# A graph layer on one core: six instead of four relations as seven half-size products, edge work re-placed

## What is computed

```python
xn = layernorm(x)
# graph part: relational mean of neighbours, R = 8
u = xn @ root + bias
for r in range(8):
    mask = (edge_type == r)
    sums = segment_sum(xn[src] * mask, dst); cnt = segment_sum(mask, dst)
    u = u + (sums / max(cnt, 1)) @ weight[r]
z = concat([u, xn], 1) @ w_gate + b_gate
h = tanh(u) * z + xn * (1 - z)
# linear attention of 16 heads: q, k, v, g, o products of 1024 x 1024
x = x + h + attention(xn)
# one LSTM cell per row: three of four gates, their x half
x = x + lstm(layernorm(x))
```

## Time and profile before

| | us |
|---|---|
| median of three runs | 2176.46 |
| fastest run | 2169.57 |
| the profiled execution | 2178.85 |
| its span, first to last instruction | 2177.1 |
| busy: TensorE | 2123.1 |
| busy: VectorE | 1307.1 |
| busy: GpSimd | 715.4 |
| busy: ScalarE | 538.5 |
| mean granted TensorE clock, of full | 0.989 |

### The profile page before, as it was taken

One profiled execution on the slowest core, in us unless ns is written; L12 is line 12 of the kernel. 1 busy time (PEld: TensorE's weight loads), 2 busy tenths in 40 slices (PEclk: granted clock), 3 DMA queues, 4 the chain that ended last, 5 costly groups with the idle time before them and its releaser, 6 DMA issues.

```text
span 2177.1 us, 25376 instructions
## 1 busy us (share of the span) xinstructions
PE 2123.1 (98%) x9562; PEld 1711.9 (79%) x9562; DVE 1307.1 (60%) x1737; ACT 538.5 (25%) x749; POOL 715.4 (33%) x631
## 2 busy tenths in 40 slices
PE   7789899989999999999999999999999999999999
PEld 6667677778888888888877778889988888788887
DVE  5565979756666666676666566773355658534233
ACT  4334354511111111100121211112232313321121
POOL 1404002026556556453635445541212353000000
PEclk9899999999999999999999999999999999999999
DMA  7887676769588988793978888964169988604102
GB/s 274 298 282 239 226 248 210 259 176 330 194 286 314 302 300 301 266 304 96 332 256 283 276 275 292 310 214 159 65 185 267 283 286 266 179 16 131 55 30 80
DMA packets 248145, 497.69 MB, mean 229 GB/s; under 512 B 39441, under 2 KB 71872, under 8 KB 248022
## 3 DMA queue, kind: packets, MB, share of 16 engines
q1 hardware_dynamic: 165782, 279.20, 39.0%
q0 software_dynamic: 65248, 191.13, 26.5%
q10 hardware_dynamic: 16992, 25.73, 3.7%
HBM read 403.60 MB, written 133.45 MB: 247 GB/s over the span
## 4 chain that ended last, share of the span: by engine, by line
PE 87%; DVE 5%; DMA 4%; issue 2%; ACT 1%; POOL 1%; SPq 0%; ACTq 0%; POOLq 0%; DVEq 0%
PE acc L1414 70%; PE acc L1385 10%; PE acc L1409 5%; DMA ax_d<-aTraw 1%; DMA y_d<-made 1%; POOL runs L2386 1%; PE acc L1322 1%; DMA xr<-in_x 1%; DVE Wlo L1710 1%; DMA made<-y_d 1%; PE misc L1307 1%; PE tp L1269 0%; DMA runs<-code_d,run_row 0%; DVE res L1781 0%; PE acc L1422 0%
## 5 line engine op out<-in xcount | busy, mean ns | idle before, releaser
L1414 PE MATMUL acc<-Whi,aThi 128*128 128x512 f32 (+1 forms) x2232 | 882.1, 395 | 0.7 <-DVE A L2139 0.6
L1414 PE MATMUL acc<-Whi,aTlo 128*128 128x512 f32 (+1 forms) x2232 | 879.1, 394 | 0.0
L1414 PE MATMUL acc<-Wlo,aThi 128*128 128x512 f32 (+1 forms) x2232 | 876.5, 393 | 0.0
L2406 POOL DMA_INDIRECT ring<-y_d,edge x390 | 477.8, 1225 | 429.2 <-DVE U L2009 138.8
L1414 PEld LDWEIGHTS acc<-Whi,aTlo 128*128 128x128 f32 (+1 forms) x2232 | 413.7, 185 | 103.5
L1414 PEld LDWEIGHTS acc<-Wlo,aThi 128*128 128x128 f32 (+1 forms) x2232 | 414.4, 186 | 102.4
L1414 PEld LDWEIGHTS acc<-Whi,aThi 128*128 128x128 f32 (+1 forms) x2232 | 413.6, 185 | 103.3 <-DVE A L2139 1.1
L1710 DVE TENSOR_TENSOR Wlo<-Wraw,Whi 128x1024 fp32r<-128x1024 f32 x176 | 218.9, 1249 | 156.4 <-ACT Whi L1440 152.8
L1385 PE MATMUL acc<-Whi,aThi 128*128 128x512 f32 (+2 forms) x560 | 230.5, 412 | 36.0 <-DVE Wlo L1710 12.1
L2009 DVE SCALAR_TENSOR_TENSOR U<-ring,edge,U 128x1024 f32<-128x1024 f32 x180 | 230.4, 1280 | 23.6 <-DMA ring<-y_d,edge 23.1
L2009 DVE SCALAR_TENSOR_TENSOR odd<-ring,edge,odd 128x1024 f32<-128x1024 f32 x170 | 217.6, 1280 | 36.7 <-DMA ring<-y_d,edge 36.2
(11 more groups left out here) (209 smaller groups left out, 1520.8 us busy)
## 6 DMA issues: line engine op xcount, KB each, us to landing
Wraw<-in_L_gnn_weight SPq DMA_DIRECT2D x80, 512.0 KB, 7.7
y_d<-res SPq DMA_DIRECT2D x80, 256.0 KB, 3.4
Whraw<-in_L_gnn_weight SPq DMA_DIRECT2D x24, 512.0 KB, 7.1
y_d<-made ACTq DMA_DIRECT2D x32, 256.0 KB
Wraw<-in_L_gnn_w_gate SPq DMA_DIRECT2D x16, 512.0 KB, 7.4
y_d<-made ACTq DMA_DIRECT2D x32, 252.0 KB
ring<-y_d,edge POOLq DMA_INDIRECT x390, 6.3
aTraw<-ax_d SPq DMA_DIRECT2D x4, 1250.0 KB, 9.7
```

The source lines that it names most:

```text
L1414: mm = nc.tensor.matmul(to, a[:, k, rows(i)], b[:, s % 2, k, :], start=start, stop=stop)
L2406: pool.indirect_dma_start(ring[:, j % RING, :], None, a, bass.IndirectOffsetOnAxis(ap=index, axis=0), bounds_check=top - 1, oob_is_err=Fal ...
```

## The change

`SEVEN` now holds six relations. There are 210 block units in place of 140, and four Y stages in place of eight; units in all are 474 in place of 444. All places that follow from it (junctions of AL, BE and DE, `SPREAD`, `SWAP`) keep their distance to their stages. `RIGHT_AT` moves from units 25 to 30 to units 44 to 50. The edges' preparation up to the reading of runs stays at its units; what follows is stretched from 61/32 to 183/64 of a unit, starts at unit 57 in place of 55, and the pieces of the tables stand 1.8 units apart in place of 0.5. GpSimd makes all its row sums before the edge codes. The sums' first half lies on units 214 to 277 (63 units, to unit 7 of the first `V_`) in place of 144 to 223 (79); the second half on 277 to 347 (70) in place of 223 to 317 (94). Both still end in the last `G_`. `y_d` keeps its two halves of four relations.

```diff
@@ -83,14 +83,14 @@
-SEVEN = list(range(HALF_R))
+SEVEN = list(range(6))
...
-STAGE += [(Y_, r, h) for r in range(HALF_R, R) for h in range(2)]
+STAGE += [(Y_, r, h) for r in range(len(SEVEN), R) for h in range(2)]
@@ -225,9 +225,10 @@
-AL_LAST, BE_FIRST, DE_FIRST = HALF_R - 1, HALF_R, STAGE.index((DE_, 0, 0))
+AL_LAST, BE_FIRST, DE_FIRST = len(SEVEN) - 1, len(SEVEN), STAGE.index((DE_, 0, 0))
-SPREAD = [(3, None, 31), (0, POS[AL_LAST, 4], 35), (1, LAST[AL_LAST], 41), (2, None, 43)]
+SPREAD = [(3, None, FIRST[AL_LAST] + 1), (0, POS[AL_LAST, 4], FIRST[AL_LAST] + 5), (1, LAST[AL_LAST], FIRST[BE_FIRST] + 1),
+          (2, None, FIRST[BE_FIRST] + 3)]
@@ -308,17 +309,17 @@
-RIGHT_AT = (25, 28, 29, 30)
+RIGHT_AT = (44, 46, 48, 50)
...
-SENDS_AT = (104, 131)
+SENDS_AT = (132, 193)
...
-    return divmod(440 + (8 * (q - 36) + k) * 61 // 32, 8)
+    return divmod(462 + (8 * (q - 36) + k) * 183 // 64, 8)
@@ -359,8 +360,8 @@
-SUMS_FROM = (place(Y_, 0, 4, HALF_R), place(R_, 0, 3))
-SUMS_TO = (place(R_, 0, 3), place(G_, 1, 7))
+SUMS_FROM = (place(Y_, 0, 4, len(SEVEN)), place(V_, 0, 7))
+SUMS_TO = (place(V_, 0, 7), place(G_, 1, 7))
@@ -1673,7 +1674,7 @@
-                            if (q, k) == edge_at(43 + 15 * h + t // 2 * 3 + t % 2, 5):
+                            if (q, k) == edge_at(44 + 20 * h + t // 2 * 3 + t % 2, 5):
                                 rank_signs(h, t)
@@ -2298,27 +2299,27 @@
-                        if (q, k) == edge_at(36 + h, 6):
+                        if (q, k) == edge_at(36 + 2 * h, 6 - 4 * h):
                             run_half(h)
-                    if (q, k) == edge_at(38, 2):
+                    if (q, k) == edge_at(39, 2):
                         run_keys()
...
-                            if (q, k) == edge_at(41 + 15 * h + t // 2 * 3 + t % 2, 1):
+                            if (q, k) == edge_at(42 + 20 * h + t // 2 * 3 + t % 2, 1):
                                 top_of(h, t)
-                        if (q, k) == edge_at(58 + 15 * h, 1):
+                        if (q, k) == edge_at(58 + 20 * h, 1):
                             ranks_whole(h)
...
-                            if (q, k) == edge_at(58 + 15 * h, 4 + 2 * piece):
+                            if (q, k) == edge_at(59 + 20 * h, 5 * piece):
                                 tables_weights(h, piece)
@@ -2470,15 +2471,13 @@
-            for t in (1, 2):
+            for t in range(1, T):
                 rows_sum(t)
             edge_codes()
...
-            for t in range(3, T):
-                rows_sum(t)
```

More of the change, by code:

```diff
@@ L1331, in beside @@
                     turn_x(TURN_AT[q])
-                if q == place(Y_, 0, 4, HALF_R) and k == 2:
+                if q == place(Y_, 0, 4, len(SEVEN)) and k == 2:
                     any_bad()
@@ L2300, in _ @@
                     for h in range(2):
-                        if (q, k) == edge_at(36 + h, 6):
+                        if (q, k) == edge_at(36 + 2 * h, 6 - 4 * h):
                             run_half(h)
-                    if (q, k) == edge_at(38, 2):
+                    if (q, k) == edge_at(39, 2):
                         run_keys()
                     for h in range(2):
-                        if (q, k) == edge_at(38 + h, 6):
+                        if (q, k) == edge_at(39 + h, 6):
                             hold_half(h)
@@ L2309, in _ @@
                         for t in range(T):
-                            if (q, k) == edge_at(41 + 15 * h + t // 2 * 3 + t % 2, 1):
+                            if (q, k) == edge_at(42 + 20 * h + t // 2 * 3 + t % 2, 1):
                                 top_of(h, t)
-                        if (q, k) == edge_at(58 + 15 * h, 1):
+                        if (q, k) == edge_at(58 + 20 * h, 1):
                             ranks_whole(h)
-                        if (q, k) == edge_at(58 + 15 * h, 2):
+                        if (q, k) == edge_at(58 + 20 * h, 2):
                             tables(h)
                         for piece in range(4):
-                            if (q, k) == edge_at(58 + 15 * h, 4 + 2 * piece):
+                            if (q, k) == edge_at(59 + 20 * h, 5 * piece):
                                 tables_weights(h, piece)
-                    if (q, k) == (place(Y_, 0, 2, HALF_R), 5):
+                    if (q, k) == (place(Y_, 0, 2, len(SEVEN)), 5):
                         columns_over()
-                    if (q, k) == (place(Y_, 0, 5, HALF_R), 2):
+                    if (q, k) == (place(Y_, 0, 5, len(SEVEN)), 2):
                         which_path()
```

## The result

| | before | after |
|---|---|---|
| median beside each other, us | 2177.85 | 2158.73 |
| ratio, with its 95% interval | | 0.9904 (0.9885 to 0.9923) |
| the profiled execution, us | 2178.85 | 2150.63 |
| its span, us | 2177.1 | 2148.8 |
| block stages, from the first to the first Y unit, us | 460.8 (140 units) | 611.0 (210 units) |

The change takes about 1% off; the prediction was 2119 with 2100 to 2155, and the median lies above that range.

A forecast was written before the change was run, and what follows sets the result against it. TensorE, busy 98% of the span, was taken as the bound. 2177.1 - 27 (products) - 33 (pauses) + 0 (edge sums) = 2117 us of span, so 2119 us, range 2100 to 2155.

The forecast's parts named there:

- Products: TensorE's matmuls: two relations change from Y stages to seven half-size products each, 27 us less, bounds 20 and 27.
- Pauses: TensorE's pauses in the block stages, before 471.2 us: four causes eased, 33 us less, bounds 5 and 50.
- GpSimd's order: First 23 block units: row sums ahead of the edge codes end SyncE's and VectorE's waits, 10 us back, bounds 0 and 17.
- The right-hand differences: Second and third block stretches: moving RIGHT_AT later avoids VectorE's wait for the store of x's sides, 10 us, bounds 3 and 14.
- The runs: VectorE's 6.9 us wait for the runs of codes shrinks with 15 units' lead instead of 13: 5 us, bounds 0 and 6.
- The tables: Block stages: table pieces spread to 1.8 units apart no longer hold up evictions, 8 of 7 + 9 us, bounds 2 and 13.
- The edge sums: Ordinary stages: gather-and-add steps squeezed to 1.80 and 1.88 us still stay hidden, 0 us, bounds 0 and 40.
- the ring's pace away from a stage's start: Ordinary stages after a stage's first four units: five gathers in flight allow a step every 1.56 us, so the plan is met.
- B: Rival, chance 0.25: the ring of gathers falls behind by a few per cent, 1.92 us a step, TensorE waits 22 us, 2141 us.
- C: Rival, chance 0.08: the ring runs throughout at 2.2 us a step as at a stage's start, TensorE waits 137 us, 2256 us.
- A: The forecast case, chance 0.55: products and pauses give 60 us and the edge sums stay hidden, 2119 us, range 2102 to 2135.
- D: Rival, chance 0.12: block-stage pauses stay because they are the DMA's; only products and 5 us count, 2147 us.

The follow-up runs named there:

- six places: Changed kernel with six places in the ring of gathers in place of five; median 2113.03 us, ratio to before 0.9703.
- four places: Changed kernel with four places in the ring of gathers in place of five; 2245.6 us in one run.
- seven places: Changed kernel with seven places in the ring of gathers in place of five; median 2108.09 us, ratio to before 0.9686.

## Why the prediction was wrong

**Products, 27 us: right.** Every BE, GA and DE stage from unit 70 on takes 27.9 us, with no excess. No run isolates this term; it closes the account.

**Pauses, 33 us: right in kind, too small; 44.8 in the trace of after, 40 to 48 by the traces with the same block stages.** By item:

1. GpSimd's order, 10 foreseen: 8 us between the traces (8.8 us at units 17 and 18 before, 0.9 after), 3 to 9 when undone or done alone. Row sum 3 starts at 34.32 us, before 45 as required.
2. The right-hand differences, 10 foreseen: 10.4 us went at the junction of AL and BE (14.6 at units 35 to 42 of before, 4.2 at 59 to 62 of after). The cause named holds in the trace of before, whose chain runs through the wait of the earlier trace rows and ScalarE behind it; of the 4.2 us that stayed, the chain of after is the storing and loading for seeds that was foreseen to stay. **The cure was not the one named**: with `RIGHT_AT` at its old units the wait returned and no time with it, and with everything else of the edges put back units 30 to 58 stayed free of pauses as well. What is left is that two more AL stages put the junction and its spreads 20 units later, away from the wait. That was not tried by itself, nor was `RIGHT_AT` moved alone in the kernel before.
3. The runs, 5 foreseen: 9.2 us were lost at units 59 to 61 of before, and in the trace of after the runs cost nothing. That was luck in part, since "no wait for runs" did not hold: six places waited 11.4 us for them, before itself 6.9. With the old places the loss there was 8 to 12 us more.
4. The tables, 8 foreseen: all 16.3 us went. The old pace brings 8.5 of them back, the first half's nearly whole; the other 8 most likely went with the place of the second half's tables. I had read their price, 7 + 9 us, and taken only half of it back. Items 3 and 4 together are what the spread is for: undoing it costs 16 to 20 us at the runs and the tables, less than the products give.

**The edge sums, 0 us (bounds 0 and 40): wrong, +43.7 us.** The failed step is the ring's pace away from a stage's start, (6.2 + 1.3 + 0.3) / 5 = 1.56 us. It was mis-sized in three terms. From an add's end to the next issue it is not 0.3 but 1.34 us: 1.49 us where GpSimd was still issuing another gather (121 of the steps 40 to 194, 1.29 us an issue), and 0.80 us even where it was free. A gather lands in 6.8, not 6.2 us, with five always in flight. And VectorE begins 0.4 us after the landing on average (at once in two steps of three, later where splits and evictions come between). (6.8 + 1.23 + 1.34 + 0.4) / 5 = 1.95 us, which is the pace of steps 40 to 195 (1.943); 1.99 over all. Most of this could be read in the trace of before. Its adds kept a cycle of 1.52 + 6.18 + 3.16 + 1.22 us, of which only 3.16 was room, so (12.08 - 3.16) / 5 = 1.78 us was the floor, against a plan of 1.80. Over its steps 40 to 195 alone, the ones that the new plan squeezes most, the same three parts were 1.60 + 6.50 + 1.22 = 9.32 us, 1.86 a step and already above the plan.

The other half of that step, 2.2 us a step at a stage's start, was misread too: 439 us over 195 steps is 2.25 us, so the earlier trace rows show the old plan's pace and not the ring's limit. In after the adds of the first four units of a stage (second Y to second R) begin 1.89 us apart, those of the other six 1.95.

The slack was also read too high. "About 11 us" holds for splits and for the evictions of R, X and G; the K stages' evictions have 4.2 us (above), and 15 of the 33.6 us of gaps over 0.3 us are there. The other 10 of the 43.7 us are the remainder; the slower clock after gaps (0.97 between 1040 and 1300 us) is in it, and gaps too short to list.

One sign was badly chosen: VectorE's waits for splits did fall from 123 us to under 40 (to 11.8), and had been listed as a sign of being right. They fell because VectorE was late.

**The rivals.** B had the mechanism and the formula: 410 x 1.987 - 765 = 50 us, against 43.7 measured. Its pace (1.92) was too low, and it had a quarter of the chance. C, the ring at 2.2 us throughout, stayed away: that pace came only with four places, which made the kernel 3.2% slower than before (one run, 2245.6 over 2176.59). A, the sums staying hidden, is what six places give: the 2119 us of the forecast stand beside the 2113.03 measured. D did not hold; the pauses went. With the measured sizes the prediction's sum is 2178.85 - 27 - 45 + 44 = 2151 us, the profiled execution's 2150.63, as it must be, since the three sizes are taken from that trace; the median is 8 us above. A's own range (to 2135) was narrower than its bounds, which reach 2178.85 - 25 = 2154.

Half a gather lands in 4.4 us, a whole one in 6.8. Drawn as a line through these two points, which were taken under unequal traffic (217 and 306 GB/s), that is 2.0 us that does not go with the bytes, and 2.4 us for 0.23 MB, some 96 GB/s for one transfer among five. The Trainium skill (DMA: Bandwidth & Descriptors, Anatomy of one DMA) has a fixed part of about 2.0 us, with which this agrees, and 436 GB/s for the rest, by an estimate 0.5 us for those bytes; under this load the runs contradict it by a factor of four to five.

## What to carry to other kernels

Size a ring of transfers by its whole cycle as the trace has it: from the release to the issue (where the issuing engine's own 1.3 us stand in a row), to the landing under the new load, to the use, and the use; only the time from landing to use is room. When work is squeezed into less time, add a place before moving the plan: here one place of 4 KB a partition made 0.970 of 0.990, and nothing at all (0.9987) in the kernel whose plan was slack. A wait that is long in a view may cost nothing (14.5 us at the right-hand differences, with the spreads 20 units away), and the same wait may lie on the chain that ended last (before, with the spreads right behind it); a burst of small instructions on an engine that is 60% busy may cost 7 us. The work that stands behind decides. Putting the old place back into the new kernel tells what it costs there, and not what it cost in the old one: for that, read the old kernel's chain.

## What the runs showed of the hardware

Indirect gathers of up to 128 rows of 4 KB: landing 6.0, 6.8, 7.1 and 7.2 us (medians) with four, five, six and seven places, while the core's traffic in the same stretch rose from 274 to 306, 318 and 328 GB/s. From four to five places the rate was held back by the number in flight; with six and seven the plan sets the pace (1.90 and 1.88 us a step), so their rates are no limit of the memory. Half the bytes gave 4.4 us and 217 GB/s. Issuing one kept GpSimd 1.26, 1.29, 1.33 and 1.35 us on average with four to seven places, and 1.11 us with five places and half the columns in each add. In after, an issue with VectorE idle for over four fifths of it took 0.99 us (50 of them, none over 1.04), an issue with VectorE busy for over half of it 1.35 us on average, so the issue is longer beside VectorE's work. From an add's end to the issue that it releases it took 0.76 us at the least. After a pause TensorE's granted clock, over the 12 to 13 us around it, was a mean of 0.71 to 0.81 (0.76 at the K stage of after), so between its two levels, 1.2 and 2.4 GHz. A pause costs more than its idle time: after the 3.82 us at 145.07 us of before, the next twelve matmuls took 5.3 us, where twelve undisturbed ones take 2.8.
